# Order of loads and splits in the prologue, narrower products for C0 and D0, and two banks for x1's groups, in a fused two-layer LoRA kernel

## The chip, the cores and the metric

One core of one Trainium2 chip. The time is device microseconds of one launch. Three runs of the kernel before took 460.31, 460.7 and 461.73 us; the median is 460.7.

## The reference, cut to what matters

x is 8 batches of 256 rows by 1024 columns, in float32. Two layers follow each other, each with a residual:

```python
x = x + L0_ffn(L0_cond(x, lang_ids))    # L0_cond: x W0^T + gated rank-16 adapters (A0, B0), top 2 of 8 experts
                                        # L0_ffn: top-1 routed adapters (route_w, A, Bw), R0 = [route_w; A]
x = x + L1_ffn(L1_cond(x, slot_ids))    # L1_cond: x W1^T + b1 + a rank-16 adapter of each batch (lora_As, lora_Bs of its slot)
                                        # L1_ffn: x Wbase^T + b_base + top-2 routed adapters (W_router, A1, B1)
```

The kernel never forms the middle of a layer. It multiplies weights with weights once: M = W1^T F, with F = [W_router; A1; Wbase]; FE = Bs^T F for the eight batches' adapters; C0 = W0^T R0^T and D0 = B0^T R0^T. Then each tile of 128 rows goes through the folded factors.

## The kernel before, in words

**Splitting.** Every operand is float32 kept as two float32r parts: ScalarE copies the raw tile to hi (`hi_half`, L567), VectorE subtracts it to get lo (`lo`, L858; `lo_in`). A product is three matmuls: hi x hi, hi x lo, lo x hi (`three`, L1339, L1340, L1341).

**Prologue, 0 to about 150 us.** TensorE computes M's rows in pairs (`m_steps`, banks 0 to 2 for even rows, 5 to 7 for odd rows), with F and the first rows of W1 loaded in parts. Then comes FE from Bs into banks 0 to 2 (`fe_done`). D0 follows: 8 steps j with B0 left and R0 right, into 136 columns of bank 7 (`d0w`), by `three`, so 24 matmuls. C0 follows: 8 tiles k of W0, each 8 steps j; a step is two matmuls, W0's hi and W0's lo, both with R0's hi and lo side by side as 272 columns (L1427); afterwards the two halves are added (`c0_half`, `c0_sum`). Then come M's remaining rows, with the first two x tiles between them.

**Queues.** Every engine's instruction order is written out by hand and kept strictly. SyncE issues nearly all transfers: F and W1's first rows, R0, W0(0), B0, A0, then the eight Bs tiles (64 KB each, their address read from a register), then x, W1, W0(1) after row 0 of M is complete, W0(2) after row 1. Behind FE it stores FE's three chunks, hi and lo (`store_fe`, L377 and L378), with W0(3) behind the second store, W0(4) behind the third and behind `d0w_done`, W0(5) behind `c0_used` 1, W0(6) behind `fe_stored` 96 (all six stores complete; its place is FE's), W0(7) behind `c0_used` 3. W0(3) lands in bs_lo_t_raw, W0(4) in b0lo_raw, W0(5) in w0s_lo_raw, W0(6) in xT_second_lo_raw. ScalarE and VectorE split R0, B0, A0 and then Bs, before they take M's row 0 out of PSUM (`fold_rows(0)`: add the identity, keep the direct part Mdir, form the factors G). FE's first matmul waits for Bs's lo and for Mdir's lo, because FE overwrites the bank of row 0 (`m_lo`).

**Main part.** Eight slots, one for each batch of two tiles. A slot holds 16 direct steps, 28 steps of seven products (Strassen-like, G and left), and, between them, small products and transposes for the gates. `main_to(n)` runs the main steps up to n, 0.62 us each. Slots 0 to 6 also carry the next batch through layer 0 (`has_a`); its last part is `ffn0`, four groups g of x1 = x + the layer-0 output, all through bank 0 (`x1w`), each behind VectorE's addition of the group before (`x1_add`, `x1_sum`). In slot 0 VectorE also takes the lo part of B1 (`b1_lo`) ahead of the second hs. In slot 7 the transpose of the first wz stands at `main_to(24)`.

Of the kernel before, what the change touches and what calls it, by code (L numbers as in the profile page):

```python
# [5 lines left out]
P = 128  # L6
# [18 lines left out]
def adaln_ffn(nc, xT, lang_ids, slot_ids, W0, R0, A0, B0, Bw, W1, b1, lora_As, lora_Bs, F0, F1, F2, b_base, B1, out):  # L25
# [11 lines left out]
    with ctx:  # L37
        def sb(name, shape, dt=F32, where=None):
            return (where or ctx).enter_context(nc.sbuf_tensor(name, shape, dt))
# [18 lines left out]
        D0lo = sb("D0lo", [P, RC], F32R)  # L58
# [111 lines left out]
        d0w_done, d0w_hi, d0w_lo = sem("d0w_done"), sem("d0w_hi"), sem("d0w_lo")  # L170
        fe_done, fe_hi, fe_lo, fe_stored = sem("fe_done"), sem("fe_hi"), sem("fe_lo"), sem("fe_stored")
# [92 lines left out]
        d0w = banks[:, 7, 0:RC]  # L264
# [7 lines left out]
        X1W_FIRST = [p0, pt, p0, pt]  # L272

# [54 lines left out]
        def _(sp):  # L328
# [28 lines left out]
            load_w0(0)  # L357
            load(b0raw[:, :], B0, b0_in)
            load(a0_part(C0raw), A0, a0_in)
            sp.wait_ge(ids_in, 32)  # L360
            for b in range(NB):
                slot = sp.value_load(ids[0:1, NB + b:NB + b + 1], min_val=0, max_val=lora_Bs.shape[0] - 1)  # L362
                load(bs_raw[:, b * P:(b + 1) * P], lora_Bs[bass.ds(slot, 1), :, :].rearrange("s p c -> p (s c)"), bs_in)
            for half in range(2):
                load(x_raw0[:, half * D:(half + 1) * D], xT[0, :, half * D:(half + 1) * D], x0_in[half])
# [3 lines left out]
            sp.wait_ge(m_done, m_count(0, 2))  # L369
            load_w0(1)  # L370
# [10 lines left out]
            store_fe(1)  # L381
            sp.wait_ge(fe_done, 3)
            load_w0(3)
            store_fe(2)
            sp.wait_ge(d0w_done, 1)
            load_w0(4)
            sp.wait_ge(c0_used, 1)
# [175 lines left out]
        def _(act):  # L563
# [122 lines left out]
            hi_half(r0_in, 16, R0Thi, R0raw, r0_hi)  # L686
            hi_half(b0_in, 16, b0hi[:, :], b0raw[:, :], b0_hi)
            hi_half(a0_in, 16, a0_part(C0hi), a0_part(C0raw), a0_hi)
# [5 lines left out]
            keep(right_raw(0, T3), m_psum(0, 2), m_hi)  # L694
            act.wait_ge(m_lo, m_lo_at(0, 3))
# [15 lines left out]
            act.wait_ge(d0w_done, 1)  # L711
            act.activation(D0hi[:, :], d0w, ACT.Copy, scale=2.0).then_inc(d0w_hi, 1)
# [142 lines left out]
        def _(dve):  # L855
# [145 lines left out]
            def x1_add(q, g, raw, bank=x1w):  # L1001

                dve.wait_ge(x1w_done, q * 4 + g + 1)
                dve.tensor_tensor(raw_quarter(raw, g), by_half(bank), raw_quarter(raw, g), ALU.add).then_inc(x1_sum, 1)  # L1004
# [121 lines left out]
            def fold_rows(s):  # L1126
                par, row, p = s % 2, M_ROWS[s], s // 2
                add_ident(s)
# [29 lines left out]
            for i in range(3, 11):  # L1158
                f_split(i)
            lo_in(r0_hi, 1, R0Tlo, R0raw, R0Thi, r0_lo)  # L1160
            lo_in(b0_hi, 1, b0lo[:, :], b0raw[:, :], b0hi[:, :], b0_lo)
            lo_in(a0_hi, 1, a0_part(C0lo), a0_part(C0raw), a0_part(C0hi), a0_lo)
            lo_in(bs_hi, 1, k_first(bs_lo_t), by_batch(bs_raw), k_first(bs_hi_t), bs_lo)
            dve.wait_ge(ident_ready, 1)
            fold_rows(0)
# [7 lines left out]
            keep_fe(2)  # L1173
            dve.wait_ge(d0w_hi, 1)
            lo(D0lo[:, :], d0w, D0hi[:, :], 2.0).then_inc(d0w_lo, 1)
# [91 lines left out]
            def slot(b, turn, has_a, has_n):  # L1267
# [9 lines left out]
                if b == 0:  # L1277
                    lo_in(b1_hi, 1, B1Tlo[:, :], B1raw[:, :], B1Thi[:, :], b1_lo, 2.0)
# [4 lines left out]
                if has_a:  # L1283
                    top1(a)
                s_sums(b, turn, (3,))
# [21 lines left out]
                if has_a:  # L1307
                    x1_add(q, 0, raw)
                    x1_add(q, 1, raw)
                    x1_add(q, 2, raw)  # L1310
                    a_part(q, 1 - turn, 0)
                keep_p167(b)
                if has_a:
                    x1_add(q, 3, raw)
                    a_part(q, 1 - turn, 1)
                    a_part(q, 1 - turn, 2)
                    a_part(q, 1 - turn, 3)
# [18 lines left out]
        def _(pe):  # L1336
# [5 lines left out]


# [73 lines left out]
            for j in range(K):  # L1417
                ins = three(d0w, split_of(b0hi, b0lo, j), (R0Thi[:, j, :], R0Tlo[:, j, :]), j == 0, j == K - 1)
            ins.then_inc(d0w_done, 1)

            for k in range(K):
                pe.wait_ge(w0_lo, k + 1)
                if k in (4, 6):
                    pe.wait_ge(c0_sum, k // 2 - 1)
                for j in range(K):
                    for n, w in enumerate(split_of(W0_HOME[k][0], W0_HOME[k][1], j)):
                        ins = pe.matmul(banks[:, C0_BANKS[k // 2] + k % 2, 0:2 * RC], w, R0T[:, j, :],  # L1427
                                        start=j == 0 and n == 0, stop=j == K - 1 and n == 1)
                ins.then_inc(c0_used, 1)
# [68 lines left out]
            def slot(b, turn, has_a, has_n, first=False):  # L1498
# [86 lines left out]
                if has_a:  # L1585
                    small0(a, main_tile, a * 2)
# [20 lines left out]
                main_to(26 if first else 22 if has_a else 24)  # L1607
# [25 lines left out]
                if has_a:  # L1633
                    pe.wait_ge(whT_lo, a + 2)
                    pe.wait_ge(y_act, b * 3 + 1)
                    for g in range(4):
                        if g:
                            pe.wait_ge(x1_sum, q * 4 + g)
                        ffn0(q, g, x1w)
                        main_to((42, 43, 44, 44)[g] if first else (39, 40, 42, 43)[g])  # L1640
                        if g < 2:
                            lora(m + 1, 1, g)
# [67 lines left out]
```

## Time and profile before

| what | value |
|---|---|
| median of three runs | 460.7 us (460.31 to 461.73) |
| the profiled execution's own time | 460.47 us |
| its span in the profile | 458.6 us |
| TensorE busy | 444.1 us, 97% of the span |
| weight loads busy (beside matmuls) | 412.3 us, 90% |
| VectorE, ScalarE, GpSimd busy | 307.7, 154.6, 68.7 us |
| granted TensorE clock | 9 tenths or more in all 40 slices |

Read it from the engine that is nearly always busy: what counts is where it waits, and what a matmul of each width costs from start to start. A matmul's recorded duration overlaps the next one; a matmul of 460 columns is recorded with 0.37 us and the next starts 0.21 us after it.

### The profile page before, as it was taken

The numbers are of one execution on the slowest core, as the hardware profiler recorded it, in microseconds if no ns is written. First come the engines' busy times: TensorE is split into PE (matmuls) and PEld (weight loads), VectorE is DVE, ScalarE is ACT, GpSimd is POOL, SyncE is SP. The second block draws the span as 40 slices with busy tenths as digits, with TensorE's granted clock in tenths as the row PEclk, the third lists the DMA queues.
The fourth block names the chain that finished last, engine by engine and source line by source line (L and its number), as shares of the span: only waits on it lengthen the run. The fifth ranks groups of instructions, "written<-read, shape, count | busy, mean of one in ns | idle before, by whom it ended". The sixth has DMA issues, their size and how long they took to land.

```text
span 458.6 us, 7837 instructions
## 1 busy us (share of the span) xinstructions
PE 444.1 (97%) x2758; PEld 412.3 (90%) x2758; DVE 307.7 (67%) x916; ACT 154.6 (34%) x325; POOL 68.7 (15%) x61
## 2 busy tenths in 40 slices
PE   4999989999999999999999999999999999999997
PEld 4988989999998988899999999999999999999986
DVE  4847486889843988388477558638837746763842
ACT  5746263212232652243233233314324323321310
POOL 2000000000003420402402302221040240220110
PEclk9999999999999999999999999999999999999999
DMA  8972661101110101112104102111310410200202
GB/s 273 387 236 122 202 226 46 48 0 48 53 46 1 56 16 50 47 63 102 46 19 142 52 1 108 56 45 63 99 46 18 148 46 10 108 2 1 109 2 91
DMA packets 16863, 37.08 MB, mean 81 GB/s; under 512 B 2615, under 2 KB 8761, under 8 KB 16830
## 3 DMA queue, kind: packets, MB, share of 16 engines
q1 hardware_dynamic: 16734, 36.66, 23.2%
q8 instruction: 18, 0.29, 0.3%
q14 instruction: 15, 0.12, 0.1%
q0 software_dynamic: 96, 0.00, 0.0%
HBM read 27.07 MB, written 9.59 MB: 80 GB/s over the span
## 4 chain that ended last, share of the span: by engine, by line
PE 76%; DVE 11%; SPq 5%; issue 3%; ACT 3%; DMA 1%; DVEq 0%; ACTq 0%
PE banks L1339 24%; PE banks L1341 23%; PE banks L1340 23%; SPq L330 4%; DVE G L858 3%; PE banks L1427 2%; PE banks L1572 2%; PE banks L1354 1%; DMA bs_lo_t_raw<-in_W_dram 1%; DVE G_raw L1118 1%; SPq L362 1%; DVE left L858 1%; ACT bs_hi_t L567 1%; DVE ws_lo L858 1%; PE banks L1481 0%
## 5 line engine op out<-in xcount | busy, mean ns | idle before, releaser
L1339 PE MATMUL banks<-G,left 128*128 128x460 f32 x224 | 88.0, 393 | 0.0
L1340 PE MATMUL banks<-G,left 128*128 128x460 f32 x224 | 82.9, 370 | 0.0
L1341 PE MATMUL banks<-G,left 128*128 128x460 f32 x224 | 82.9, 370 | 0.0
L1339 PE MATMUL banks<-WbThi,ws_hi 128*128 128x460 f32 (+1 forms) x192 | 67.1, 349 | 6.6 <-DVE WbTlo L858 6.2
L515 POOL TENSOR_TENSOR xTlo<-x_raw,xThi 128x512 fp32r<-128x512 f32 x28 | 37.9, 1373 | 202.6 <-DVE hg L916 107.5
L1341 PE MATMUL banks<-WbThi,ws_lo 128*128 128x460 f32 (+1 forms) x192 | 65.8, 342 | 0.0
L1340 PE MATMUL banks<-WbTlo,ws_hi 128*128 128x460 f32 (+1 forms) x192 | 65.6, 342 | 0.0
L567 ACT ACTIVATE left<-x_raw 128x512 fp32r<-128x512 f32 x64 | 38.7, 627 | 59.9 <-DVE x_raw L1004 29.3
L1339 PEld LDWEIGHTS banks<-G,left 128*128 128x128 f32 x224 | 42.5, 190 | 4.5 <-DVE wzTlo L858 0.3
L1341 PEld LDWEIGHTS banks<-G,left 128*128 128x128 f32 x224 | 42.0, 188 | 4.7
L1339 PEld LDWEIGHTS banks<-WbThi,ws_hi 128*128 128x128 f32 x192 | 36.8, 192 | 10.0 <-issue 7.2
L1340 PEld LDWEIGHTS banks<-G,left 128*128 128x128 f32 x224 | 42.4, 189 | 2.6
L1004 DVE TENSOR_TENSOR x_raw<-banks,x_raw 128x512 f32<-128x512 f32 x32 | 22.1, 692 | 28.0 <-PE banks L1341 27.1
L1340 PEld LDWEIGHTS banks<-WbTlo,ws_hi 128*128 128x128 f32 x192 | 36.9, 192 | 2.9
L1341 PEld LDWEIGHTS banks<-WbThi,ws_lo 128*128 128x128 f32 x192 | 36.8, 192 | 2.6
L1035 DVE TENSOR_TENSOR ybuf<-banks,ybuf 128x460 f32<-128x460 f32 x48 | 29.6, 630 | 11.4 <-PE banks L1341 10.6
L1339 PE MATMUL banks<-Mdir,left 128*128 128x256 f32 x128 | 36.5, 285 | 0.2 <-DVE left L858 0.2
L1340 PE MATMUL banks<-Mdir,left 128*128 128x256 f32 x128 | 35.9, 281 | 0.0
L1341 PE MATMUL banks<-Mdir,left 128*128 128x256 f32 x128 | 35.9, 281 | 0.0
L515 POOL TENSOR_TENSOR left<-x_raw,left 128x512 fp32r<-128x512 f32 x16 | 20.7, 1314 | 99.4 <-DVE hg L916 74.5
L858 DVE SCALAR_TENSOR_TENSOR left<-x_raw,left 128x512 fp32r<-128x512 f32 x48 | 32.3, 686 | 2.7 <-ACT left L567 1.9
L1341 PE MATMUL banks<-C0hi,xTlo 128*128 128x272 f32 x112 | 32.3, 288 | 0.0
(208 smaller groups left out, 964.7 us busy)
## 6 DMA issues: line engine op xcount, KB each, us to landing
x_raw<-in_xT_dram SPq DMA_DIRECT2D x16, 512.0 KB, 3.8
out_dram<-ybuf SPq DMA_DIRECT2D x14, 512.0 KB, 2.7
WbTlo_raw<-in_F_dram SPq DMA_DIRECT2D x8, 460.0 KB, 8.2
x_raw<-in_W_dram SPq DMA_DIRECT2D x6, 512.0 KB, 3.3
ws_lo_raw<-in_W_dram SPq DMA_DIRECT2D x3, 512.0 KB, 5.2
w0s_lo_raw<-in_W_dram SPq DMA_DIRECT2D x2, 512.0 KB, 9.3
Fbuf<-fe_hi_dram SPq DMA_DIRECT2D x16, 64.0 KB
ws_lo_raw<-in_W_dram SPq DMA_DIRECT2D x3, 256.0 KB, 4.6
```

Of the source, the lines that this page charges most:

```text
L330: return sp.dma_start(dst, src).then_inc(s, 16)
L362: slot = sp.value_load(ids[0:1, NB + b:NB + b + 1], min_val=0, max_val=lora_Bs.shape[0] - 1)
L515: return gp.tensor_tensor(out_, a, b, ALU.subtract)
L567: act.activation(dst, src, ACT.Copy).then_inc(ready, 1)
L858: return dve.scalar_tensor_tensor(out=out_, in0=src, scalar=scale, in1=hi.bitcast(F32), op0=ALU.mult, op1=ALU.subtract)
L1004: dve.tensor_tensor(raw_quarter(raw, g), by_half(bank), raw_quarter(raw, g), ALU.add).then_inc(x1_sum, 1)
L1035: return dve.tensor_tensor(ybuf[tile][:, y0:y0 + n], bank, base, ALU.add).then_inc(ready, 1)
L1339: pe.matmul(out_, l[0], r[0], start=start, stop=False, **kw)
L1340: pe.matmul(out_, l[0], r[1], start=False, stop=False, **kw)
L1341: return pe.matmul(out_, l[1], r[0], start=False, stop=stop, **kw)
L1427: ins = pe.matmul(banks[:, C0_BANKS[k // 2] + k % 2, 0:2 * RC], w, R0T[:, j, :], start=j == 0 and n == 0, stop=j == K - 1 and n == 1)
L1572: pe.matmul(y, hsT[half][:, :], Fbuf[:, s], start=False, stop=True, skip_group_check=True)\
```

## The change

On SyncE the eight Bs loads come directly after R0; W0(0), B0 and A0 follow; W0(1) comes ahead of x, W1(2) and b1. Between the stores of FE, W0(3) moves ahead of the second one and W0(4) ahead of the third. ScalarE and VectorE split Bs and take out M's row 0 before they split R0, B0 and A0. D0 and C0 use a new helper, `with_both`: the left's hi with R0's hi and lo (272 columns), the left's lo with R0's hi alone (136 columns). D0's halves are now added by ScalarE and VectorE as C0's are. In slot 0, B1's lo moves behind `top1`. x1's groups alternate between bank 3 (`p0`) and bank 0; in slot 7 the transpose of wz moves from step 24 to step 26.

```diff
@@ scratch and semaphores
-        D0lo = sb("D0lo", [P, RC], F32R)
+        D0lo, D0raw = twin("D0lo", [P, RC])
+        d0w_half, d0w_sum = sem("d0w_half"), sem("d0w_sum")
-        d0w = banks[:, 7, 0:RC]
+        d0w = banks[:, 7, 0:2 * RC]
+        X1W = [p0, x1w, p0, x1w]
@@ SyncE
             load(R0raw, R0, r0_in)
-            load_w0(0)
-            load(b0raw[:, :], B0, b0_in)
-            load(a0_part(C0raw), A0, a0_in)
             sp.wait_ge(ids_in, 32)
             for b in range(NB):
                 ...
+            load_w0(0)
+            load(b0raw[:, :], B0, b0_in)
+            load(a0_part(C0raw), A0, a0_in)
+            sp.wait_ge(m_done, m_count(0, 2))
+            load_w0(1)
             for half in range(2):
                 ...
-            sp.wait_ge(m_done, m_count(0, 2))
-            load_w0(1)
             sp.wait_ge(m_done, m_count(1, 2))
             load_w0(2)
...
             store_fe(0)
-            store_fe(1)
             sp.wait_ge(fe_done, 3)
             load_w0(3)
-            store_fe(2)
+            store_fe(1)
             sp.wait_ge(d0w_done, 1)
             load_w0(4)
+            store_fe(2)
             sp.wait_ge(c0_used, 1)
             load_w0(5)
@@ ScalarE
-            hi_half(r0_in, 16, R0Thi, R0raw, r0_hi)
-            hi_half(b0_in, 16, b0hi[:, :], b0raw[:, :], b0_hi)
-            hi_half(a0_in, 16, a0_part(C0hi), a0_part(C0raw), a0_hi)
             hi_half(bs_in, 16 * NB, k_first(bs_hi_t), by_batch(bs_raw), bs_hi)
             act.wait_ge(m_ident, 1)
             keep(direct(0, M_ROWS[0]), m_psum(0, 0), m_hi)
             keep(right(0, B11)[0], m_psum(0, 1), m_hi)
             act.wait_ge(m_done, m_count(0, 2))
             keep(right_raw(0, T3), m_psum(0, 2), m_hi)
+            hi_half(r0_in, 16, R0Thi, R0raw, r0_hi)
+            hi_half(b0_in, 16, b0hi[:, :], b0raw[:, :], b0_hi)
+            hi_half(a0_in, 16, a0_part(C0hi), a0_part(C0raw), a0_hi)
...
-            act.wait_ge(d0w_done, 1)
-            act.activation(D0hi[:, :], d0w, ACT.Copy, scale=2.0).then_inc(d0w_hi, 1)
+            hi_half(d0w_done, 1, D0raw[:, :], d0w[:, RC:2 * RC], d0w_half)
+            act.wait_ge(d0w_sum, 1)
+            act.activation(D0hi[:, :], D0raw[:, :], ACT.Copy, scale=2.0).then_inc(d0w_hi, 1)
@@ VectorE
+            dve.wait_ge(ident_ready, 1)
+            add_ident(0)
+            lo_in(bs_hi, 1, k_first(bs_lo_t), by_batch(bs_raw), k_first(bs_hi_t), bs_lo)
+            fold_rows(0)
             lo_in(r0_hi, 1, R0Tlo, R0raw, R0Thi, r0_lo)
             lo_in(b0_hi, 1, b0lo[:, :], b0raw[:, :], b0hi[:, :], b0_lo)
             lo_in(a0_hi, 1, a0_part(C0lo), a0_part(C0raw), a0_part(C0hi), a0_lo)
-            lo_in(bs_hi, 1, k_first(bs_lo_t), by_batch(bs_raw), k_first(bs_hi_t), bs_lo)
-            dve.wait_ge(ident_ready, 1)
-            fold_rows(0)
...
+            dve.wait_ge(d0w_half, 1)
+            dve.tensor_tensor(D0raw[:, :], d0w[:, 0:RC], D0raw[:, :], ALU.add).then_inc(d0w_sum, 1)
             dve.wait_ge(d0w_hi, 1)
-            lo(D0lo[:, :], d0w, D0hi[:, :], 2.0).then_inc(d0w_lo, 1)
+            lo(D0lo[:, :], D0raw[:, :], D0hi[:, :], 2.0).then_inc(d0w_lo, 1)
@@ VectorE, slot
-                if b == 0:
-                    lo_in(b1_hi, 1, B1Tlo[:, :], B1raw[:, :], B1Thi[:, :], b1_lo, 2.0)
...
                 hs_part(m + 1, 1)
                 if has_a:
                     top1(a)
+                if b == 0:
+                    lo_in(b1_hi, 1, B1Tlo[:, :], B1raw[:, :], B1Thi[:, :], b1_lo, 2.0)
...
-                    x1_add(q, 0, raw)
-                    x1_add(q, 1, raw)
-                    x1_add(q, 2, raw)
+                    for g in range(3):
+                        x1_add(q, g, raw, X1W[g])
@@ TensorE
+            def with_both(out_, l, r, start, stop):
+                n = out_.shape[-1] // 2
+                pe.matmul(out_, l[0], r, start=start, stop=False, skip_group_check=True)
+                return pe.matmul(out_[:, 0:n], l[1], r[:, 0:n], start=False, stop=stop, skip_group_check=True)
...
             for j in range(K):
-                ins = three(d0w, split_of(b0hi, b0lo, j), (R0Thi[:, j, :], R0Tlo[:, j, :]), j == 0, j == K - 1)
+                ins = with_both(d0w, split_of(b0hi, b0lo, j), R0T[:, j, :], j == 0, j == K - 1)
...
                 for j in range(K):
-                    for n, w in enumerate(split_of(W0_HOME[k][0], W0_HOME[k][1], j)):
-                        ins = pe.matmul(banks[:, C0_BANKS[k // 2] + k % 2, 0:2 * RC], w, R0T[:, j, :],
-                                        start=j == 0 and n == 0, stop=j == K - 1 and n == 1)
+                    ins = with_both(banks[:, C0_BANKS[k // 2] + k % 2, 0:2 * RC], split_of(W0_HOME[k][0], W0_HOME[k][1], j),
+                                    R0T[:, j, :], j == 0, j == K - 1)
...
                 if has_a:
+                    pe.wait_ge(x1_sum, b * 4 + 3)
                     small0(a, main_tile, a * 2)
-                main_to(26 if first else 22 if has_a else 24)
+                main_to(26 if first else 22 if has_a else 26)
                 turn_small(wz_ready, m + 1, pt_wz, wz[:, :], twz_done)
...
-                    pe.wait_ge(y_act, b * 3 + 1)
                     for g in range(4):
-                        if g:
-                            pe.wait_ge(x1_sum, q * 4 + g)
-                        ffn0(q, g, x1w)
+                        if g == 1:
+                            pe.wait_ge(y_act, b * 3 + 1)
+                        elif g > 1:
+                            pe.wait_ge(x1_sum, q * 4 + g - 1)
+                        ffn0(q, g, X1W[g])
```

## Rows read from the trace of the kernel before

**Rows 1.** The page, busy time, share and instructions of each engine

```profile
PE 444.1 (97%) x2758; PEld 412.3 (90%) x2758; DVE 307.7 (67%) x916; ACT 154.6 (34%) x325; POOL 68.7 (15%) x61
```

**Rows 2.** Waits of TensorE: who waited for whom, us in total, times, longest

```profile
PE banks L1339 <- DVE WbTlo L858: 6.2, 2, 5.3
PE banks L1427 <- DVE bs_lo_t L858: 1.3, 1, 1.3
...
PE banks L1339 <- DVE x_raw L1004: 0.2, 1, 0.2
```

**Rows 3.** Timeline of TensorE at FE's start: start, duration, instruction, [idle before <-releaser]

```profile
33.78 0.36 PE L1341 MATMUL banks<-WbThi,ws_lo 128*128 128x460 f32 x1
35.07 0.35 PE L1339 MATMUL banks<-WbThi,bs_hi_t 128*128 128x240 f32 x1 [0.92 <-DVE Mdir L858]
```

**Rows 4.** Timelines of ScalarE and VectorE, 29 to 35 us

```profile
29.26 2.29 ACT L567 ACTIVATE bs_hi_t<-bs_raw 128x1024 fp32r<-128x1024 f32 x1 [1.91 <-DMA bs_raw<-in_lora_Bs_dram]
...
31.58 2.21 DVE L858 SCALAR_TENSOR_TENSOR bs_lo_t<-bs_raw,bs_hi_t 128x1024 fp32r<-128x1024 f32 x1 [2.91 <-ACT bs_hi_t L567]
...
34.51 0.41 DVE L858 SCALAR_TENSOR_TENSOR Mdir<-banks,Mdir 128x240 fp32r<-128x240 f32 x1 [0.43 <-ACT Mdir L674]
```

**Rows 5.** Timeline of SyncE's queue: start and duration of issues

```profile
9.70 6.22 SPq L330 DMA_DIRECT2D w0s_lo_raw<-in_W_dram  x1
...
18.26 9.45 SPq L330 DMA_DIRECT2D bs_raw<-in_lora_Bs_dram  x8
...
51.03 0.46 SPq L330 DMA_DIRECT2D bs_lo_t_raw<-in_W_dram  x1
...
52.03 0.43 SPq L378 DMA_DIRECT2D fe_lo_dram<-fe_keep_lo  x1
...
56.93 0.33 SPq L330 DMA_DIRECT2D xT_second_lo_raw<-in_W_dram  x1
```

**Rows 6.** Timeline of TensorE through D0 and C0

```profile
50.14 0.28 PE L1339 MATMUL banks<-R0T,b0hi 128*128 128x136 f32 x1
...
50.48 0.34 PE L1427 MATMUL banks<-R0T,w0s_hi 128*128 128x272 f32 x1
...
57.99 0.40 PE L1427 MATMUL banks<-R0T,bs_hi_t 128*128 128x272 f32 x1 [1.29 <-DVE bs_lo_t L858]
...
59.98 0.29 PE L1427 MATMUL banks<-R0T,bs_lo_t 128*128 128x272 f32 x1
61.01 0.39 PE L1427 MATMUL banks<-R0T,b0hi 128*128 128x272 f32 x1 [0.74 <-DVE b0lo L858]
```

**Rows 7.** DMA issues, 46 to 62 us: KB each, median us from issue to landing

```profile
bs_lo_t_raw<-in_W_dram SPq DMA_DIRECT2D x1, 512.0 KB, 4.6
b0lo_raw<-in_W_dram SPq DMA_DIRECT2D x1, 512.0 KB, 5.6
w0s_lo_raw<-in_W_dram SPq DMA_DIRECT2D x1, 512.0 KB, 6.4
xT_second_lo_raw<-in_W_dram SPq DMA_DIRECT2D x1, 512.0 KB, 3.7
```

**Rows 8.** Timeline of VectorE, lo of W0(4) and of W0(6)

```profile
59.73 1.23 DVE L858 SCALAR_TENSOR_TENSOR b0lo<-b0lo_raw,b0hi 128x1024 fp32r<-128x1024 f32 x1 [0.50 <-ACT b0hi L567]
...
63.49 1.22 DVE L858 SCALAR_TENSOR_TENSOR xT_second_lo<-xT_second_lo_raw,xT_second_hi 128x1024 fp32r<-128x1024 f32 x1
```

**Rows 9.** Timelines of VectorE and TensorE in slot 0

```profile
169.04 2.35 DVE L858 SCALAR_TENSOR_TENSOR ws_lo<-ws_lo_raw,ws_hi 128x1024 fp32r<-128x1024 f32 x1 [0.63 <-ACT ws_hi L815]
...
171.76 0.32 PE L1577 MATMUL banks<-ident,hs 128*96 128x128 f32 x1 [0.48 <-DVE hs L858]
...
184.00 0.63 DVE L1035 TENSOR_TENSOR ybuf<-banks,ybuf 128x460 f32<-128x460 f32 x1
...
197.51 0.48 PE L1339 MATMUL banks<-ws_hi,wzThi 128*128 128x460 f32 x1 [0.18 <-DVE ybuf L1035]
```

**Rows 10.** Timeline of TensorE in slot 7

```profile
438.36 0.33 PE L1354 MATMUL banks<-ident,wz 128*128 128x128 f32 x1 [0.59 <-DVE wz L916]
```

More of the change, by code:

```diff
@@ L999, in wzT_part, with x1_add @@
                 lo(wzTlo[:, :], pt_wz, wzThi[:, :]).then_inc(wzT_lo, 1)
-            def x1_add(q, g, raw, bank=x1w):
+            def x1_add(q, g, raw, bank):
                 dve.wait_ge(x1w_done, q * 4 + g + 1)
@@ L1127, in fold_rows @@
                 par, row, p = s % 2, M_ROWS[s], s // 2
-                add_ident(s)
+                if s > 0:
+                    add_ident(s)
                 if s > 1:
@@ L1313, in slot @@
                 if has_a:
-                    x1_add(q, 3, raw)
+                    x1_add(q, 3, raw, X1W[3])
                     a_part(q, 1 - turn, 1)
```

## The prediction

> **What bounds the kernel now.** The page comes first: TensorE is busy for 444.1 of 458.6 us, VectorE for 307.7 [rows 1]. So time is gained only where TensorE waits or where it has less to do. The list of waits shows where it waits: 6.2 us on the first lo parts at the very start, then small waits [rows 2]. The timeline of TensorE puts each at its place: before FE [rows 3], twice inside C0 [rows 6], at the second hs and at the end of slot 0 [rows 9], at the first wz of slot 7 [rows 10]. The slots between show none. The recorded idle time of such a wait is less than it costs, because a matmul's recorded duration overlaps the next one: after 33.78 the next 460-column matmul would have started 0.21 us later, at 33.99, and started at 35.07, so a wait with 0.92 us of idle costs 1.08 [rows 3]. The same 0.16 us is added to the others.
>
> **FE's start.** FE waits for Mdir's lo, at 34.51 [rows 4]. The chain before it: the eight Bs loads are issued from 18.26 to 27.71 behind W0(0), whose issue alone held SyncE's queue for 6.22 us [rows 5]; they land at 29.2, ScalarE's hi takes 2.29 us, VectorE's lo 2.21 us, then the identity, Mdir's hi and lo [rows 4]. From landing to FE are 5.84 us. In the changed kernel the Bs loads are issued in the place of W0(0). At worst the 6.22 us hold falls on the first of them; then the rest, at 9.45/8 = 1.2 us each, are issued by about 25.5 and landed by about 27.5. FE finds everything ready if the last Bs lands by 33.99 - 5.84 = 28.15. The whole 1.08 us goes, and 0.07 us of restart behind it. R0, B0, A0 and their splits move behind, W0(1) moves ahead of x. They are wanted by D0, which starts 24 x 0.113 us before 50.48 [rows 6], at 47.8, so a dozen microseconds cover them; the splits are the same number of instructions as before. Without that cover each microsecond that W0(1) came late would be one on TensorE, because row 1 of M is taken out behind its split. The first batch's x and W1(2) come later by one transfer; their splits stand behind those of W0(5) and later tiles, so that costs nothing.
>
> **D0.** 24 matmuls of 136 columns become 8 of 272 and 8 of 136. Three of 136 take from 50.14 to 50.48, so 0.113 us each [rows 6]. From 50.48 the three W0 tiles would have ended at 57.99 - 1.29 - 0.16 = 56.54, 48 matmuls in 6.06 us, 0.126 us each [rows 6]. D0 costs 24 x 0.113 = 2.71 before and 8 x (0.126 + 0.113) = 1.91 after: 0.80 us less. The added copy, sum and third instruction of D0's split (some 0.3 us each) lie on ScalarE and VectorE where both wait for W0(3); if W0(3) were there, they would delay its split by about 1 us.
>
> **C0.** 64 of its 128 matmuls shrink from 272 to 136 columns: 64 x 0.013 = 0.83 us. Half the columns do not halve the time, since 136 columns already take 0.113 us, with a weight load before each. The Trainium skill (TensorE: Matmul & The Clock Gate, Back-to-back issue gap) gives 128 columns 134 cycles, about 56 ns, when isolated; by that the two edits would bring 0.4 and 3.4 us more. Its section on LDWEIGHTS puts 107 ns on 128 columns of weights, which is what rows 6 show as a floor. The sum goes by the rows.
>
> **The late tiles of W0.** The two waits cost 1.29 + 0.16 and 0.74 + 0.16, and each is followed by a restart with 0.10 us more [rows 6]: 2.55 us in all. W0(3) was issued at 51.03, behind the second store, which waited for VectorE; now it only waits for FE's end, 1.15 us ahead of D0's old start, 46.7. With 4.6 us to landing [rows 7], ScalarE's hi of 1.05 and VectorE's lo of 1.23 us [rows 8] it is ready by 53.7. TensorE, running 1.15 us ahead and with a shorter D0, wants W0(k) at 48.5 + 1.91 k: W0(3) at 54.2. Good. The next ones are closer. W0(4) is issued at about 48.9, lands after 3.7 to 5.6 us [rows 7], is ready at 54.9 to 56.8 and wanted at 56.1. W0(5), issued at 50.7 behind the third store, lands after 3.7 to 6.4 us: ready at 56.7 to 59.4, wanted at 58.0. W0(6) waits for all stores: before, from the last issue's end at 52.46 to 56.93, 4.5 us [rows 5]; now from about 50.4, so issued at 54.9 or a little earlier, landed 3.7 us later, ready near 60.9, wanted at 59.9. VectorE sets a second limit: from the start of W0(4)'s lo to the end of W0(6)'s it needs 64.6 - 59.7 = 4.9 us [rows 8]. Between nothing and some 2.1 us of new waits I take 0.5, near the low end: the transfers are issued two microseconds further apart from each other than before, and the stores that lay around W0(3) are out of its way. The Trainium skill (DMA: Bandwidth & Descriptors, Queues, rings and completion order) says that each DMA engine takes descriptors in ring order and that a completion lands only after that engine's earlier writes; that speaks for W0(3) and against W0(4) and W0(5), which now have a store ahead. No row here separates ring order from plain bandwidth.
>
> **After C0** TensorE is without a wait up to slot 0, so what is gained until then stays, as long as VectorE and ScalarE, whose chains there start from TensorE's results, follow.
>
> **Slot 0.** The second hs stands behind B1's lo, which took from 169.04 to 171.31, nearly twice its 1.23 us [rows 8, 9]. Moving it frees the wait of 0.48 + 0.12 us [rows 9]. But VectorE is busy almost without a gap up to the ybuf sum at 184.00, which TensorE needs for its next product, and its work stays: it would stand idle for 1 us more in front of hs, and get back about as much because B1's lo runs alone later. I count 0.1 us of the 0.6.
>
> **x1 in two banks.** Only slot 0 shows a wait for `x1_add`, 0.17 + 0.15 us, and the next product then waits for a ybuf sum at 197.51 anyway [rows 2, 9]: that sum hangs on the third group, whose time does not change. Nothing is gained; the new wait ahead of `small0` is for an addition long done. **Slot 7**: 0.59 + 0.16 = 0.75 us [rows 10]; two main steps (1.25 us) now cover VectorE's wz, and its lo part is wanted four steps later, which is enough.
>
> **The sum**: 1.15 + 0.80 + 0.83 + 2.55 - 0.5 + 0.1 + 0.75 = 5.7 us, from 460.47 for the profiled execution to 454.8; the median of the runs is 0.2 above it, so 455.0.
>
> **Rivals.**
> 1. The late tiles stay late: W0(4) to W0(6) cost the full 2.1 us. For it: 4.6 to 6.4 us to landing, and 4.5 us for the stores. Against it: fewer transfers stand at once. 456.6. Chance 0.25.
> 2. Slot 0 keeps its 0.6 us, because something behind hs has more room than I see; 454.5. Chance 0.12.
> 3. The narrow matmuls don't save: a sequence that alternates 272 and 136 columns is in no row, and the pitch may stay at 0.126. Then D0 gives 0.7 and C0 nothing; 455.9. Chance 0.08.
> 4. The Bs loads are held up: the queue that let W0(0) wait 6.22 us is asked for eight register-addressed loads at that point. If each waits until the transfers ahead have landed, the last Bs lands near 32; FE then starts 4 us later than forecast. Up to 458.8. Chance 0.04.
> 5. The other side, by the same place: FE's start follows the last Bs's landing by 5.84 us, so past 28.15 each microsecond is lost. The kernel is slower than before by 0.3% (462.1) from a landing at 35.3 on, four times the hold that rows 5 show. Chance 0.03.
> 6. Narrow matmuls as isolated ones, at 59 ns: TensorE would reach the late tiles sooner and wait for them, so of 3.8 us about 0.5 is left; 454.5. The page named under C0 has that rule; rows 6 speak against it. Chance 0.02.
>
> **How the numbers follow.** The forecast itself has 0.46. Its range takes in the bounds of the late tiles and slot 0's; low end 453.8, if no new wait appears and slot 0 gives all; high end 457.2, with the full new waits and no gain from narrow matmuls. Cases outside are rivals 4 and 5. Measurements of this kernel agree to about 0.3%, 1.4 us: every case but the fifth and part of the fourth is faster by more. Faster 0.94, same 0.03, slower 0.03.
>
> **What would show it.** Right: no idle before FE's first matmul, which starts at 34.0; D0 in 1.9 us; W0 tiles 1.91 us apart; W0(3) issued near 46.9 and without a wait; M's row 2, behind C0, some 4.8 us earlier; the wait at hs gone and a longer one near 184; no wait at wz in slot 7. Wrong: idle before FE, tiles of W0 2.0 us apart, or waits on W0(4) to W0(7) of more than 1 us together.

## The result, and the profile after the change

The changed kernel took 457.44 us (median of 10 runs, 456.6 to 460.12) beside 460.83 us (10 runs, 460.21 to 462.19): a ratio of 0.9932 over all the runs, 95% interval 0.9918 to 0.9946 (the two medians alone give 0.9926). It is faster by 3.4 us, not by the 5.7 us forecast, and lies 0.2 us above the range's high end. Its profiled execution took 457.89 us with a span of 456.1, so against the 460.47 that the sum started from it shows only 2.6 us.

The page, busy time of each engine [rows 1], and TensorE's waits [rows 2]:

```profile
PE 443.6 (97%) x2750; PEld 412.5 (90%) x2750; DVE 306.9 (67%) x917; ACT 155.0 (34%) x326; POOL 68.7 (15%) x61
```

```profile
PE banks L1345 <- DVE WbTlo L861: 5.6, 2, 5.3
...
PE banks L1345 <- DVE ybuf L1038: 0.6, 1, 0.6
PE banks L1353 <- DVE xT_second_lo L861: 0.5, 1, 0.5
PE banks L1353 <- DVE b0lo L861: 0.5, 1, 0.5
PE banks L1353 <- DVE w0s_lo L861: 0.5, 1, 0.5
PE banks L1366 <- DVE wz L919: 0.3, 1, 0.3
...
PE banks L1366 <- DVE hg L919: 0.2, 1, 0.2
```

The waits for Mdir, W0(3), hs and slot 7's wz are gone. Three of 0.5 us stand inside C0: the one at W0(4) (b0lo) was 0.74 before, those at W0(5) (w0s_lo) and W0(6) (xT_second_lo) are new. Slot 0 has three others, at wz, hg and ybuf. TensorE's timeline at FE's start and through D0 and C0 [rows 3, 6]:

```profile
35.67 0.27 PE L1345 MATMUL banks<-WbThi,bs_hi_t 128*128 128x240 f32 x1
...
48.36 0.29 PE L1353 MATMUL banks<-R0T,b0hi 128*128 128x272 f32 x1
...
50.22 0.34 PE L1353 MATMUL banks<-R0T,w0s_hi 128*128 128x272 f32 x1
50.39 0.22 PE L1354 MATMUL banks<-R0T,w0s_lo 128*128 128x136 f32 x1
50.46 0.34 PE L1353 MATMUL banks<-R0T,w0s_hi 128*128 128x272 f32 x1
...
58.48 0.39 PE L1353 MATMUL banks<-R0T,b0hi 128*128 128x272 f32 x1 [0.50 <-DVE b0lo L861]
...
61.07 0.39 PE L1353 MATMUL banks<-R0T,w0s_hi 128*128 128x272 f32 x1 [0.47 <-DVE w0s_lo L861]
...
63.69 0.39 PE L1353 MATMUL banks<-R0T,xT_second_hi 128*128 128x272 f32 x1 [0.51 <-DVE xT_second_lo L861]
...
67.53 0.33 PE L1345 MATMUL banks<-WbThi,ws_hi 128*128 128x240 f32 x1
```

The same two ends in the kernel before, D0's first matmul and the first one behind C0:

```profile
47.84 0.23 PE L1339 MATMUL banks<-R0T,b0hi 128*128 128x136 f32 x1
...
69.14 0.27 PE L1339 MATMUL banks<-WbThi,ws_hi 128*128 128x240 f32 x1
```

FE starts without a wait, yet 0.60 us later than before. D0 takes 50.22 - 48.36 = 1.86 us (50.48 - 47.84 = 2.64 before); a pair of C0 takes 0.24 us (50.22 to 50.46); C0 ends at 67.53, where the next product starts. SyncE's queue [rows 5] and the landings [rows 7]:

```profile
11.47 13.30 SPq L332 DMA_DIRECT2D bs_raw<-in_lora_Bs_dram  x8
...
48.56 0.34 SPq L332 DMA_DIRECT2D bs_lo_t_raw<-in_W_dram  x1
...
50.41 0.34 SPq L332 DMA_DIRECT2D b0lo_raw<-in_W_dram  x1
...
51.32 0.63 SPq L380 DMA_DIRECT2D fe_lo_dram<-fe_keep_lo  x1
52.32 0.34 SPq L332 DMA_DIRECT2D w0s_lo_raw<-in_W_dram  x1
57.47 0.34 SPq L332 DMA_DIRECT2D xT_second_lo_raw<-in_W_dram  x1
```

```profile
bs_lo_t_raw<-in_W_dram SPq DMA_DIRECT2D x1, 512.0 KB, 4.0
b0lo_raw<-in_W_dram SPq DMA_DIRECT2D x1, 512.0 KB, 5.7
w0s_lo_raw<-in_W_dram SPq DMA_DIRECT2D x1, 512.0 KB, 6.4
xT_second_lo_raw<-in_W_dram SPq DMA_DIRECT2D x1, 512.0 KB, 3.2
```

W0(3) lands in 4.0 us and is in time. W0(4) and W0(5) (b0 and w0s) land in 5.7 and 6.4 us, the slow end of what was bounded. W0(6), which waits for all stores, is issued 5.5 us after the last store's issue ended at 51.95, where 4.5 us was taken. ScalarE and VectorE [rows 4, 8, 9], ScalarE's line first:

```profile
26.13 2.30 ACT L569 ACTIVATE bs_hi_t<-bs_raw 128x1024 fp32r<-128x1024 f32 x1 [5.27 <-DMA bs_raw<-in_lora_Bs_dram]
```

```profile
30.57 0.42 DVE L861 SCALAR_TENSOR_TENSOR Mdir<-banks,Mdir 128x240 fp32r<-128x240 f32 x1
...
57.20 1.23 DVE L861 SCALAR_TENSOR_TENSOR b0lo<-b0lo_raw,b0hi 128x1024 fp32r<-128x1024 f32 x1 [0.98 <-ACT b0hi L569]
59.79 1.23 DVE L861 SCALAR_TENSOR_TENSOR w0s_lo<-w0s_lo_raw,w0s_hi 128x1024 fp32r<-128x1024 f32 x1 [1.36 <-ACT w0s_hi L569]
60.93 1.22 DVE L861 SCALAR_TENSOR_TENSOR ws_lo<-x_raw,ws_hi 128x1024 fp32r<-128x1024 f32 x1
...
62.41 1.22 DVE L861 SCALAR_TENSOR_TENSOR xT_second_lo<-xT_second_lo_raw,xT_second_hi 128x1024 fp32r<-128x1024 f32 x1
...
168.54 0.19 DVE L1085 CAST hs<-banks 128x32 fp32r<-128x32 f32 x1 [1.65 <-PE banks L1588]
```

The Bs were landed by 26.1 us and Mdir's lo done at 31.0: 4.7 us early. W0(4)'s and W0(5)'s lo are behind waits of 0.98 and 1.36 us for their hi halves, that is for the landings. W0(6) itself had landed by 60.7; its lo stands behind W1(2)'s (60.93).

**Where the time went.** I compare four stretches by TensorE's starts, in us:

| stretch | before | after | forecast | found |
|---|---|---|---|---|
| to FE's start | 35.07 | 35.67 | -1.15 | +0.60 |
| FE to D0 | 12.77 | 12.69 | 0 | -0.08 |
| D0 to C0's end | 21.30 | 19.17 | -3.7 | -2.13 |
| C0's end to the last matmul (455.23, 452.76) | 386.09 | 385.23 | -0.85 | -0.86 |

The forecast of the third is 0.80 + 0.83 + 2.55 - 0.5. The last stretch came out as forecast. The second wait at hs is gone, VectorE idled 1.65 us before it, and TensorE pays at wz, hg and ybuf instead. Two stretches need an explanation: the start, and the late tiles.

### The profile page after: what moved, and what is told of

Same layout as the page of the kernel before. It is cut to its first block, busy times and chain, and to the rows that moved or that the text cites. A ratio compares the mean times of both kernels' runs of the same rounds, so it can differ in the third digit from the quotient of the medians.

```text
span 456.1 us, 7819 instructions
## 1 busy us (share of the span) xinstructions
PE 443.6 (97%) x2750; PEld 412.5 (90%) x2750; DVE 306.9 (67%) x917; ACT 155.0 (34%) x326; POOL 68.7 (15%) x61
## 4 chain that ended last, share of the span: by engine, by line
PE 86%; DVE 8%; DMA 3%; issue 1%; ACT 1%; SPq 1%; DVEq 0%; ACTq 0%
PE banks L1345 27%; PE banks L1347 27%; PE banks L1346 27%; DVE G L861 2%; PE banks L1583 2%; DMA w0s_lo_raw<-in_W_dram 1%; DMA WbTlo_raw<-in_F_dram 1%; PE banks L1353 1%; PE banks L1366 1%; DVE left L861 1%; SPq L332 1%; DVE ws_lo L861 0%; PE banks L1354 0%; PE banks L1492 0%; DVE G_raw L1121 0%
```

## The experiments

Eighteen experiments ran on five chips, each beside the kernel before; some repeat a kernel. Start, FE and C0 stretch come from the one profiled execution of each. "Start" is the start of the first 460-column matmul, behind 48 matmuls of 240 columns, whose instructions are the same in both kernels; "C0 stretch" is D0's first matmul to C0's end.

| run | us (range) | ratio, 95% | start | FE | C0 stretch |
|---|---|---|---|---|---|
| before | 460.83 | | 13.98 | 35.07 | 21.30 |
| e1 before again | 460.94 (460.13-462.41) | 1.0003 (0.9989-1.0018) | 15.16 | 35.26 | 21.17 |
| after | 457.44 (456.6-460.12) | 0.9932 (0.9918-0.9946) | 15.55 | 35.67 | 19.17 |
| e2 | 456.88 (455.71-458.66) | 0.9916 (0.9891-0.9942) | 14.17 | 34.30 | 18.96 |
| e2c | 456.91 (455.91-458.81) | 0.9922 (0.9898-0.9946) | 14.78 | 34.89 | 18.47 |
| e3 | 457.04 (456.33-458.06) | 0.9922 (0.9902-0.9941) | 14.65 | 34.77 | 18.39 |
| e4 | 456.66 (456.09-459.03) | 0.9917 (0.9892-0.9941) | 15.23 | 35.25 | 18.44 |
| e5 | 458.32 (457.75-459.93) | 0.9954 (0.9939-0.9969) | 15.06 | 35.65 | 19.77 |
| e6 | 457.56 (one run) | | 15.15 | 35.17 | 18.17 |
| e7 | 455.65 (one run) | | 14.28 | 34.30 | 18.14 |
| e8 | 457.33 (456.71-457.69) | 0.9924 (0.9911-0.9937) | 15.37 | 35.38 | 19.24 |
| e9 | 455.28 (455.03-456.08) | 0.9882 (0.9868-0.9896) | 14.86 | 34.91 | 17.81 |
| e9b | 457.42 (454.98-458.65) | 0.9923 (0.9900-0.9946) | 13.96 | 34.06 | 17.44 |
| e9c | 455.88 (455.31-456.81) | 0.9896 (0.9876-0.9917) | 14.85 | 34.97 | 17.49 |
| e10 | 456.39 (454.96-457.88) | 0.9901 (0.9884-0.9918) | 17.23 | 37.35 | 17.14 |
| e10b | 456.06 (455.83-457.19) | 0.9899 (0.9880-0.9919) | 14.05 | 34.16 | 18.87 |
| e11 | 456.51 (456.12-457.19) | 0.9914 (0.9900-0.9927) | 14.99 | 35.09 | 18.31 |
| e12 | 461.49 (460.64-462.36) | 1.0016 (1.0006-1.0027) | 14.01 | 34.95 | 21.72 |
| e15 | 456.45 (456.08-457.40) | 0.9907 (0.9888-0.9927) | 15.04 | 35.17 | 18.07 |
| e16 | 456.42 (455.69-458.68) | 0.9912 (0.9889-0.9934) | 14.49 | 34.61 | 18.06 |

**e1, e2, e2c: both kernels again.**

> 

> The kernel before, unchanged. Theory: the 1.57 us by which the profiled execution of after was late at 14 us (its first 460-column matmul at 15.55 instead of 13.98) is an accident of the first transfers and comes in both kernels; this one's first 460-column matmul then starts anywhere from 13.9 to 16, ratio 1.000. Rival: the change itself moves the first 14 us; then this one starts at 13.9 to 14.1 again, and every variant of after stays above 15.

> 

> The kernel after, unchanged. Theory (accident): ratio 0.991 to 0.995 as before, first 460-column matmul between 13.9 and 16, and waits at W0(4), W0(5) and W0(6) of about 0.5 us each whatever the start is. Rival (the change moves the start): first 460-column matmul above 15 again.

> 

> The changed kernel once more, beside e9c on one chip. Late-tile theory: W0(4) and W0(5) behind a store each land in 4.7 to 5.7 and 5.3 to 6.4 us, D0 to C0's end 18.1 to 19.2 us; median 456.5 to 457.4, depending on the pace of the first 14 us.

In e1 FE had no wait at all, with the code of before:

```profile
35.06 0.37 PE L1341 MATMUL banks<-WbThi,ws_lo 128*128 128x460 f32 x1
35.26 0.32 PE L1339 MATMUL banks<-WbThi,bs_hi_t 128*128 128x240 f32 x1
```

TensorE was ready 1.27 us later than in the first profile (33.99), most of it because its start was at 15.16 instead of 13.98. So the wait of [rows 3] belonged to one early execution. e1 starts at 15.16 and e2 at 14.17: the start moves in both kernels, and the rival (the change moves it) is out. The 48 matmuls of 240 columns show where the time goes, first in the kernel before, then after, then in e2c:

```profile
8.77 0.36 PE L1340 MATMUL banks<-WbTlo,ws_hi 128*128 128x240 f32 x1
8.97 0.28 PE L1341 MATMUL banks<-WbThi,ws_lo 128*128 128x240 f32 x1
...
11.21 0.35 PE L1339 MATMUL banks<-WbThi,ws_hi 128*128 128x240 f32 x1 [0.95 <-DVE WbTlo L858]
...
13.98 0.37 PE L1339 MATMUL banks<-WbThi,ws_hi 128*128 128x460 f32 x1
```

```profile
12.08 0.54 PE L1345 MATMUL banks<-WbThi,ws_hi 128*128 128x240 f32 x1 [0.29 <-DVE WbTlo L861]
...
13.48 0.32 PE L1345 MATMUL banks<-WbThi,ws_hi 128*128 128x240 f32 x1
13.64 0.27 PE L1346 MATMUL banks<-WbTlo,ws_hi 128*128 128x240 f32 x1
...
15.55 0.37 PE L1345 MATMUL banks<-WbThi,ws_hi 128*128 128x460 f32 x1
```

```profile
12.01 0.35 PE L1345 MATMUL banks<-WbThi,ws_hi 128*128 128x240 f32 x1 [1.52 <-DVE WbTlo L861]
```

They start 0.21 us apart, then 0.11: up to about 9.0 us in before, up to 13.6 in after, and in e10 up to 17.0. But the slow pace is only a part of it. The last 24 of the 48 wait for the lo of a further part of F (WbTlo), which comes at 11.21 in before, 12.08 in after, 12.01 in e2c; from there to the start are 2.77, 3.47 and 2.77 us. So of the 1.57 us by which after starts later, 0.87 is this arrival and 0.70 the pace; e2c's start of 14.78 has no slow matmul in that group and is late by the arrival alone. In e10 the pace made it 5.08 us. Why the lo comes later is not shown. The Trainium skill (TensorE: Matmul & The Clock Gate, Part 1) says that the number of matmuls at the low clock differs between runs of one kernel and should not be fitted. These traces agree (14 slow ones in before, about 30 in after and e1).

**e3: wide products.** The second matmul of each pair goes back to 272 columns, in C0 (64 of them) and in D0's pairs (8):

```diff
-  return pe.matmul(out_[:, 0:n], l[1], r[:, 0:n], start=False, stop=stop, ...)
+  return pe.matmul(out_, l[1], r, start=False, stop=stop, ...)
```

> 

> After, but the second matmul of with_both takes both halves (272 columns), so D0 and C0 hold lo x lo again. Theory: the late tiles bound C0 from W0(4) on, so that only D0 and the first four tiles show the wider matmuls in full (8 x 0.013 + 32 x 0.013 = 0.5 us) and the rest (0.4 us) shortens the waits at W0(4) to W0(6): 0.3 to 0.6 us slower than after. Rival: the narrow matmuls count in full, 0.9 us slower.

The C0 stretch is 18.39, in the middle of the six profiles with the changed kernel's C0 (18.14 to 19.17), and C0 has no recorded wait; on e2's chip the median is 0.2 us above e2's. This speaks for the theory (what TensorE computes longer it waits less) and against the full 0.9 us, but does not measure the share: W0(4) and W0(5) landed in 4.6 and 5.1 us here, earlier than in any of the six (4.7 to 5.7 and 5.3 to 6.4).

**e4: the old order of stores** (`store_fe(1)` ahead of W0(3), `store_fe(2)` ahead of W0(4)):

```diff
             store_fe(0)
+            store_fe(1)
             sp.wait_ge(fe_done, 3)
             load_w0(3)
-            store_fe(1)
+            store_fe(2)
             sp.wait_ge(d0w_done, 1)
             load_w0(4)
-            store_fe(2)
```

> 

> After, with W0(3) behind the second store and W0(4) behind the third, as before. Theory: W0(3)'s wait of some 1.3 to 1.6 us comes back, but W0(4) and W0(5) are then reached later and wait less; since the last tiles are bound by their landing and by the chain of splits either way, the end of C0 moves by less than W0(3)'s wait: 0.3 to 1.2 us slower than after. Rival: the order gives its whole price, 1.5 us or more slower; or the stores behind W0(3) and W0(4) are what makes W0(4) to W0(6) late, and this is no slower at all.

W0(3)'s wait did not come back: one wait of 0.91 us stands at W0(4), the others vanish, the stretch is 18.44, and the median (456.66) is 0.2 us below e2's on the same chip. The expected 0.3 to 1.2 us are missing, and the rival's second half (no slower at all) came out. W0(3) was issued at 48.81 although it stood behind the second store, since that store went out at 47.96 instead of 50.18: with the early front the order of stores moves the wait and gains nothing. In e5, which has the new order and the old front, W0(3) has no wait either, so either edit alone removes it.

**e5: the old front.** Bs behind R0, W0(0), B0 and A0 again, on SyncE, ScalarE and VectorE; W0(1) behind x:

```diff
+            load_w0(0)
+            load(b0raw[:, :], B0, b0_in)
+            load(a0_part(C0raw), A0, a0_in)
             sp.wait_ge(ids_in, 32)
...
-            load_w0(0)
-            load(b0raw[:, :], B0, b0_in)
-            load(a0_part(C0raw), A0, a0_in)
```

> 

> After, with the loads and splits of Bs back behind R0, B0 and A0, and W0(1) behind x. Theory from the four profiles so far: before hid the accident of the first 14 us, because FE waited for Bs in any case (FE at 35.1 and 35.3 with the first 460-column matmul at 13.98 and 15.16); after has FE 20.1 us behind that matmul. So FE stands at 35.1 to 35.3 here whatever the start, and the median is only 0.1 to 0.8 us above after's, with less spread. Rival: the reordering gives its whole 1.15 us in the median.

458.32 us, about 1.1 above the changed kernel's runs (457.22 over all 22) and 1.0 above e8 on the same chip. That is outside the expected 0.1 to 0.8 and as much as the rival's 1.15, but not by the rival's path: FE came at 35.65, 20.59 us behind the start instead of 20.12, with a wait of 0.32, so only 0.47 us lie there. The rest is in C0 (19.77): store 1 waited for fe_lo until 51.3, and W0(4) was issued at 52.18, 3.75 us behind D0's start instead of 2.05.

**e6, e7: slot 7, and slot 0 with x1.** e6 has `main_to(24)` again in slot 7; e7 has B1's lo ahead of the second hs, and x1's groups in one bank, with their old waits:

```diff
-                main_to(26 if first else 22 if has_a else 26)
+                main_to(26 if first else 22 if has_a else 24)
```

```diff
-        X1W = [p0, x1w, p0, x1w]
+        X1W = [x1w, x1w, x1w, x1w]
...
+                if b == 0:
+                    lo_in(b1_hi, 1, B1Tlo[:, :], B1raw[:, :], B1Thi[:, :], b1_lo, 2.0)
```

> 

> The changed kernel with the one number of slot 7 put back: main_to(24) ahead of the last wz. The forecast's term says that the two main steps cover VectorE's work: the wait of about 0.6 us at the first wz of slot 7 comes back and the stretch from C0's end to the last matmul is 385.25 + 0.75 = 386.0 us, the 386.1 of the kernel before. Rival: the 0.86 us that this stretch lost came from slot 0 and x1; then it stays at 385.3.

> 

> The changed kernel with slot 0 and x1 as before: B1's lo ahead of the second hs, x1's groups in one bank. My forecast gave these two 0.1 us: the wait at the second hs (0.48 us before) is back, the waits for ybuf behind it are smaller by nearly as much, and the stretch from C0's end to the last matmul grows from 385.25 by 0 to 0.1 us. Rival 2: slot 0's 0.6 us was kept by the change; then that stretch grows by 0.5 to 0.6 us.

From C0's end to the last matmul e6 took 386.32 us, e7 385.32, the changed kernel 385.23 to 385.26, the kernel before 386.09 and 386.12. Slot 7's number is worth 1.06 us when it is taken out of the changed kernel, and 0.78 when it is all of the slots' edits that is in (e7 against before; 0.75 forecast). Slot 0 and x1 together bring 0.06 to 0.09 beside it (0.1 forecast), which is within the scatter of the profiles that share the new slots (385.20 to 385.33), and cost 0.2 without it (e6 against before): slot 7's wait is 0.79 us in e6, 0.59 before. Why is not shown. Rival 2, 0.6 us kept in slot 0, is out by both. The waits, e6's (slot 0's and slot 7's wz) and then e7's, with hs back and ybuf small:

```profile
PE banks L1366 <- DVE wz L919: 1.1, 2, 0.8
```

```profile
PE banks L1588 <- DVE hs L861: 0.5, 1, 0.5
...
PE banks L1345 <- DVE ybuf L1038: 0.2, 1, 0.2
```

In these two, on another chip, W0(4) and W0(5) landed in 4.7 to 4.8 and 5.3 us, and only W0(6)'s wait stayed: C0 stretch 18.1 to 18.2.

**e8: W1(2)'s split behind W0(6)'s**, on ScalarE and VectorE:

```diff
-            w1_split(2)
             c0_add(1)
             w0_split(6)
...
+            w1_split(2)
```

> 

> After, with the split of W1(2) behind that of W0(6) on ScalarE and VectorE. Theory: W0(6) had landed before its split began; its wait (0.5 us recorded) comes from the split of W1(2), 1.13 us of VectorE, in front of it. The wait at W0(6) goes, those at W0(4) and W0(5) stay; C0 ends 0.5 to 0.7 us earlier against its W0(0), and the median is 0.3 to 0.7 us below after's. Rival: W0(6) waits for its landing behind the stores; then nothing changes.

No gain (457.33, stretch 19.24), where 0.3 to 0.7 us were expected: the waits at W0(4) and W0(5) stayed at 0.42 and 0.37, and the wait of W0(6) went to W0(7), whose lo then stood behind W1(2)'s.

**e9, e9b, e9c: W0(3) fetched ahead of the stores**, into a buffer that is free early (the first x tile moves behind, W0(6) gets Bs's place and no longer waits for the stores):

```diff
+            load_w0(3)
...
-            sp.wait_ge(fe_done, 3)
-            load_w0(3)
...
-            sp.wait_ge(fe_stored, 96)
+            sp.wait_ge(fe_done, 3)
```

> 

> After, with W0(3) loaded into x_raw0's place before FE (the first x tiles are loaded later), W0(6) into Bs's place without waiting for FE's stores. Theory: with one transfer less between FE's end and W0(7), W0(4) and W0(5) land about 1 us earlier; the waits at W0(4) and W0(5) shrink to 0.3 us or less together, W0(6)'s 0.5 us, from the split of W1(2), stays. Median 0.8 to 1.5 us below after's. Rival: landing takes 5 to 6 us because of the stores' own time; then W0(4) and W0(5) wait as in after.

> 

> The kernel of e9_w0_3_early once more, for the comparison with e15 on one chip. W0(3) is fetched ahead of the stores, W0(4) and W0(5) land in about 4.1 to 5 us, and one wait of 0.5 us at W0(6) is left: D0 to C0's end 17.8 us (19.0 in the changed kernel as it is), median 455.3.

> 

> W0(3) fetched ahead of the stores, third time. D0 to C0's end 17.4 to 17.8 us. If that stretch alone differs, the median is 0.7 to 1.4 us below e2c_after; if the scatter of the start (1 to 3 us) is what the medians show, the two medians are within 0.5 us of each other, though the stretch in the profile is shorter.

The C0 stretch falls to 17.44 to 17.81. The waits at W0(4) and W0(5) are gone in all three; W0(6)'s, which was to stay at 0.5 us, is 0.49, none and 0.19. Landings of W0(4) and W0(5) in e9b:

```profile
b0lo_raw<-in_W_dram SPq DMA_DIRECT2D x1, 512.0 KB, 4.2
w0s_lo_raw<-in_W_dram SPq DMA_DIRECT2D x1, 512.0 KB, 4.6
```

Over all its runs the median is 455.88 (15 runs) against 457.22 (22 runs of the changed kernel), and on one chip (e9c, e2c) 455.88 against 456.91. Resampling the pooled runs puts the difference of the medians at 0.1 to 2.2 us. It is the lowest pooled median found, with e10's (456.23 over 10 runs) not clear of it. e9b, on a third chip, had the fastest single run of its comparison (454.98) and a median of 457.42 from the same code, against 455.3 expected.

**e10, e10b: also the third store and W1(2)'s split behind W0(6)**:

```diff
-            store_fe(2)
             sp.wait_ge(c0_used, 1)
             load_w0(5)
...
+            store_fe(2)
```

> 

> As e9, with the split of W1(2) behind that of W0(6), and the third store behind W0(6)'s load. Theory: no wait of more than 0.2 us is left in C0; it ends 17.2 us after D0's start (1.9 + 8 x 1.91) and the median is 1.5 to 2.1 us below after's, 455 or less. Rival: the gain is given back later, by VectorE, which reaches the first gates no earlier.

> 

> The kernel of e10_w0_3_early_w1_late once more: W0(3) early, the third row's fold and the second split of W1 behind W0(6). No wait is left in C0: D0 to its end 17.1 us, and with a start that is not slowed through all of its first 18 us (the first 460-column matmul at 14.2 to 15.5) a span of 453 to 454 and a median of 454.6 to 455.3, not above e9b by more than 0.2.

(The text for e10b names the third row's fold; it is the third store that moved.) e10 has no wait in C0, and its stretch is 17.14 us, the 17.2 of my sum before new waits. Its whole start ran at the slow pace, and it still was at 456.39. e10b did not repeat the stretch, and its median of 456.06 is above the expected 454.6 to 455.3: W0(5), issued together with W0(6), landed in 6.5 us (4.4 in e16, same order of transfers), TensorE waited 1.25 us, and the stretch was 18.87.

```profile
w0s_lo_raw<-in_W_dram SPq DMA_DIRECT2D x1, 512.0 KB, 6.5
```

**e15, e16: e9 and e10 with the wide products**, the edit of e3:

> 

> e9 with the wide products of C0 put back (272 columns in all 128 of its matmuls). Theory A (late tiles bound C0's end): TensorE comes later at each tile, the wait of 0.5 us at W0(6) shrinks, and D0 to C0's end grows by 0.83 - 0.5 = 0.3 us, 18.1. Theory B (the narrow products are worth their 0.83 us as soon as tiles are mostly there): 18.6 and a median 0.8 us above e9b.

> 

> e10 with the wide products of C0. Here no wait is left to swallow them, so both theories say the same, and only the term is tested: 64 matmuls x 0.013 = 0.83 us more from D0 to C0's end (18.0 against 17.1) and in the median. If the narrow products do not save (rival 3 of the prediction), it stays at 17.1.

e16, without a wait, has a stretch of 18.06 against e10's 17.14: 72 narrow matmuls are worth 0.92 us when no tile is late, 0.013 us each as forecast. Of it 0.16 is in D0 (2.01 against 1.85) and 0.76 in C0 (0.83 forecast). e15 has 18.07 against 17.44 to 17.81, so 0.3 to 0.6 us of it, between theory A and theory B. The 272-column matmuls of e16 start 0.12 to 0.13 us apart:

```profile
49.32 0.29 PE L1357 MATMUL banks<-R0T,w0s_hi 128*128 128x272 f32 x1
49.44 0.29 PE L1358 MATMUL banks<-R0T,w0s_lo 128*128 128x272 f32 x1
```

In the medians this is lost: e10b 456.06 and e16 456.42, e9b 457.42 and e15 456.45, with ranges that overlap.

**e11, e12: warm-up matmuls**, on the changed kernel and on the one before:

```diff
+            pe.wait_ge(ident_ready, 1)
+            for _ in range(8):
+                pe.matmul(pt_h1, ident[:, :], ident[:, :], start=True, stop=True)
```

> 

> The changed kernel with eight fp32 matmuls of the identity on itself into a free bank ahead of TensorE's first wait. In all runs so far the first matmuls of 240 columns run at 0.21 us each up to 9.0 to 13.6 us, then at 0.11, and the first 460-column matmul starts between 13.98 and 17.23. Theory A: the slow pace is TensorE's clock after idleness, the warm-up ends it earlier, that matmul starts by 13.5 to 14.3, FE at 33.6 to 34.4, and the median comes down by 1 to 1.5 us to some 455.7. Theory B: the pace is set by something else (the first loads, the chip's throttle), the warm-up changes nothing: 456.7 to 457.4, the spread as before.

> 

> The kernel before with the same eight warm-up matmuls. FE waits there for the split of Bs, which is ready at 35.1 whenever TensorE comes. Under both theories the time stays within 0.3 us of the kernel before (460.8); under A the wait ahead of FE grows to the 0.9 us of the first profile or more and FE still starts at 35.1.

The pace followed theory A at first: after the warm-up, from 1.5 to 5.3 us, the 240-column matmuls ran 0.11 to 0.13 us apart from 5.8 us on (6.4 in e12). But the start did not come earlier (14.99 and 14.01): now TensorE waited for the loads and splits of Wb and ws, and in e11 the clock fell again. The windows of TensorE, columns: stretch, its length and busy time (matmuls), granted clock, DMA share, GB/s; e11, then e12:

```profile
6.40:9.00 2.60, 1.02 (x8) 1.00 0.99 362
9.00:11.30 2.30, 2.30 (x12) 0.56 1.03 411
```

```profile
6.40:9.00 2.60, 2.02 (x16) 1.00 1.00 377
9.00:11.30 2.30, 1.08 (x11) 1.00 1.02 407
```

TensorE was busy for 1.02 of 2.60 us and then ran at the 1.2 GHz level for most of the next stretch, at the same 0.21 us per matmul as the slow starts. In e12 it was busy for 2.02 us and stayed at 2.4 GHz. e11's median, 456.51, lies between the two theories' ranges (some 455.7, and 456.7 to 457.4) and decides nothing. The kernel before got 0.7 us slower with the warm-up (ratio 1.0016), outside my 0.3, though FE came at 34.95 with 0.78 us of idle, near what theory A had; why is not shown beyond a wait of 1.71 us at W0(3), 1.17 to 1.29 without the warm-up.

## Why the prediction was off

- **FE's start, 1.15 us: the first step that failed.** The path was right: the Bs did land by 26.1 us, before the 28.15 needed; rivals 4 and 5 are out, and FE had no wait. What failed is the cost put on the old wait: I took TensorE's readiness (33.99) from one execution, whose start (13.98) is within 0.02 us of the earliest of all twenty profiles. In the fifteen profiles of changed kernels without a warm-up FE starts between 34.06 and 37.35 (median 34.91), against 35.07 and 35.26 before: about 0.25 us. Two profiles of before are few; an estimate that takes FE there as the later of 35.07 and 20.1 us behind the start, over the fifteen starts, gives 0.3. Taking the Bs loads back (e5) costs about 1.1 us, of which 0.47 is at FE and more than that in C0.
- **New waits in C0, 0.5 us: the second.** In six profiles with the changed kernel's C0 (after, e2, e2c, e6, e7, e11) the stretch exceeds the 17.14 of no wait by 2.03, 1.82, 1.33, 1.03, 1.00 and 1.17, mean 1.4. Rival 1's size (2.1) is reached in the profile of after alone. I took the low end because the transfers are further apart; the rows at hand (5.6 and 6.4 us) were the better guide, and the waits of 1.48 us recorded at W0(4) to W0(6) are the mark of being wrong that I had named.
- **D0, 0.80:** right, 1.86 us for 1.91, and 0.78 less than before. **C0's narrow products, 0.83:** right as a price (0.76 in C0, e16 against e10), but where tiles are late a part of it is swallowed (e15, and by its lack of waits e3); the rule for isolated matmuls (rival 6) and rival 3 are both out. The old waits of 2.55 us did go, if what is left at W0(4) is counted as new; that W0(3)'s went is not owed to the order of stores alone, as the forecast had it (e4).
- **Slot 0 and x1, 0.1:** 0.06 to 0.09 when undone, so not contradicted, but too small to be told from the scatter of 0.13 us; the mechanism named (hs's wait goes, ybuf's grows) is what e7 shows. **Slot 7, 0.75:** right, 0.78 by itself and 1.06 in the changed kernel.
- Of the marks, M's row 2 was forecast 4.8 us earlier; with C0's end it came only 1.6 earlier (67.53 for 69.14), because 1.75 of the missing 3.2 us lie ahead of FE and 1.55 between D0 and C0's end.
- The high end of the range, 457.2, was also added up wrongly: full new waits and no gain from narrow matmuls leave 1.15 + 0.69 + 2.55 - 2.1 + 0.1 + 0.75 = 3.1 us, which is 457.5. VectorE's 4.9 us from W0(4)'s lo to W0(6)'s is 5.0 by rows 8 (64.71 - 59.73); neither changes the forecast.

With 0.25 in place of 1.15 and 1.4 in place of 0.5 the sum is 3.9 us; e2 against e1, on one chip, gave 4.1, and the pooled runs 3.6. What stays open is why the landings, the arrival of F's last part and the length of the slow pace differ so much between executions of the same code (W0(5): 5.3 to 6.4 us).

## What to carry to other kernels

A wait measured in one profile is the difference of two arrivals; before it enters a sum, ask how much each arrival moves from run to run, above all behind the start. A saving in an engine's work ahead of a late tile is only worth what the tile leaves: fetch the tile earlier first, then count the saving. Where a load must share its time with stores, take the landing time from rows with stores around them, not from the quiet ones.

## What the runs showed of the hardware that I had not expected

- The start differs by up to 3.3 us (13.96 to 17.23) for the same 48 matmuls. Part of it is when their last operands come; part is how long TensorE stays at the pace of its 1.2 GHz level: the last 24 took 2.77 us at the fast pace and 5.08 in e10, where 22 of them were slow. The granted-clock column reads 1.00 there in the runs without a warm-up, and 0.56 in e11 at the same pace: that column did not show the first slow stretch.
- A 136-column matmul behind a 272-column one started the next 0.07 us later, but the wide one started it 0.17 us before: the pair took 0.24 us, the 0.126 + 0.113 us of the two widths by themselves in [rows 6]. Narrowing one of two saved 0.013 us, not half.
- In the six profiles with the changed kernel's C0, W0(3), ahead of the second and third store, landed in 4.0 to 4.2 us; W0(4) and W0(5), each behind a store, in 4.7 to 6.4, though all are 512 KB. A store ahead is not enough for that: in e9, e9b and e9c W0(4) stands behind the same second store, but W0(3) has been fetched long before, and it landed in 4.1 to 4.2.
